# Attention and mixture-of-experts block: probabilities exchanged between SBUF quadrants for two groups at once, products four periods behind their scores

## The reference

```python
x = L0_attn_x
xn = _layernorm(x, axis=-1)
x = x + _L0_attn_ref(xn, ...) + _L0_ffn_ref(xn, ...)
# attention, 16 heads of 64, latent of 64:
q = x @ wq.T;  kv_latent = x @ w_kv_down.T;  k = kv_latent @ w_k_up.T;  v = kv_latent @ w_v_up.T
q = q * cos + _rotate_half(q) * sin;  k = k * cos + _rotate_half(k) * sin
scores = q @ k.T / 8, causal;  out = softmax(scores) @ v @ wo.T
```

## Time and profile before

| | us |
|---|---|
| median of 3 runs | 654.88 |
| lowest, highest | 654.70, 661.92 |
| the profiled execution | 649.8 |
| its span | 648.0 |
| TensorE busy in it | 557.0 |
| VectorE, ScalarE, GpSimd busy | 421.3, 391.6, 195.0 |

### The profile page before, as it was taken

One profiled execution on the slowest core, in us unless ns is written; L12 is line 12 of the kernel. 1 busy time (PEld: TensorE's weight loads), 2 busy tenths in 40 slices (PEclk: granted clock), 3 DMA queues, 4 the chain that ended last, 5 costly groups with the idle time before them and its releaser, 6 DMA issues.

```text
span 648.0 us, 13735 instructions
## 1 busy us (share of the span) xinstructions
PE 557.0 (86%) x4914; PEld 398.8 (62%) x4914; DVE 421.3 (65%) x921; ACT 391.6 (60%) x1036; POOL 195.0 (30%) x271
## 2 busy tenths in 40 slices
PE   2899999689988998799979988897889888877883
PEld 2666776446666666566656666675666656655663
DVE  6685364577775777477767776775777768654650
ACT  2562322356775676566666776774677767766771
POOL 3024030113432443133324432432343333211121
PEclk9899999789998999899999999998999999988996
DMA  9300014236767677666777777776768766876752
GB/s 256 106 1 1 1 22 109 69 94 203 185 193 199 208 188 195 184 186 194 207 191 221 188 201 214 212 192 187 211 195 222 191 205 182 210 205 194 208 194 73
DMA packets 63124, 108.45 MB, mean 167 GB/s; under 512 B 10561, under 2 KB 50385, under 8 KB 62929
## 3 DMA queue, kind: packets, MB, share of 16 engines
q1 hardware_dynamic: 60496, 106.13, 59.3%
q10 hardware_dynamic: 2560, 1.45, 0.9%
HBM read 47.78 MB, written 42.99 MB: 140 GB/s over the span
## 4 chain that ended last, share of the span: by engine, by line
PE 67%; DVE 13%; issue 9%; ACT 5%; DMA 4%; SPq 1%; DVEq 0%; POOLq 0%; ACTq 0%; POOL 0%
PE ps L452 21%; PE ps L413 20%; DVE prob_l L777 7%; PE ps L329 5%; PE ps L399 4%; PE ps L383 4%; DVE prod L657 3%; PE ps L463 3%; PE ps L437 2%; PE ps L331 2%; ACT prob_l L588 2%; ACT scaled L491 1%; DMA scratch<-zig 1%; PE ps L332 1%; PE ps L385 1%
## 5 line engine op out<-in xcount | busy, mean ns | idle before, releaser
L413 PE MATMUL ps<-qk 64*128 64x512 f32 (+3 forms) x768 | 160.6, 523 | 35.8 <-DVE negmax L777 34.4
L491 ACT ACTIVATE scaled<-ps,rden 128x128 f32<-128x128 f32 x256 | 73.2, 369 | 131.8 <-PE ps L463 131.8
L777 DVE CUSTOM_DVE_ANT_0 prob_l<-ps,mask 128x1024 f32<-128x1024 f32 (+3 forms) x128 | 126.0, 1022 | 39.1 <-PE ps L413 39.0
L837 POOL TENSOR_TENSOR roped<-prod 128x256 f32<-128x256 f32 x64 | 47.0, 735 | 321.8 <-DVE prod L657 321.8
L588 ACT ACTIVATE prob_l<-prob_l,negmax 128x1024 f32<-128x1024 f32 (+3 forms) x128 | 126.1, 1000 | 17.3 <-DVE negmax L777 17.3
L413 PEld LDWEIGHTS ps<-qk 64*128 64x128 f32 x768 | 64.4, 188 | 96.4 <-DVE negmax L777 47.5
L846 POOL TENSOR_TENSOR acc<-acc,scaled 128x256 f32<-128x256 f32 x128 | 93.0, 727 | 88.4 <-ACT scaled L491 83.2
L657 DVE TENSOR_TENSOR prod<-ps,rope 128x1024 f32<-128x1024 f32 x64 | 78.3, 1223 | 62.6 <-PE ps L332 31.8
L452 PE MATMUL ps<-fastT,lat 128*64 128x128 f32 x1280 | 88.9, 288 | 25.8 <-ACT slowT L491 11.6
L452 PEld LDWEIGHTS ps<-fastT,lat 128*64 128x64 f32 x1280 | 72.9, 142 | 54.3 <-issue 32.5
L790 DVE STREAM_TRANSPOSE zig<-prob_l 128x640 f32<-128x640 f32 x128 | 100.3, 822 | 0.0
(11 more groups left out here) (121 smaller groups left out, 593.4 us busy)
## 6 DMA issues: line engine op xcount, KB each, us to landing
scratch<-zig SPq DMA_DIRECT2D x64, 640.0 KB, 4.4
fastT<-scratch SPq DMA_DIRECT2D x256, 160.0 KB, 3.3
qk<-roped SPq DMA_DIRECT2D x64, 256.0 KB, 5.3
acc<-x SPq DMA_DIRECT2D x2, 512.0 KB, 5.4
rope<-c_rope SPq DMA_DIRECT2D x1, 1024.0 KB, 11.8
out<-acc SPq DMA_DIRECT2D x2, 512.0 KB, 4.1
wq_raw<-wq ACTq DMA_DIRECT2D x1, 512.0 KB, 7.3
wo_raw<-wo ACTq DMA_DIRECT2D x1, 512.0 KB, 8.5
```

Of the source, the lines that this page charges most:

```text
L413: mm = nc.tensor.matmul(to, qk[p][half, 0, rows], qk[p][half, 1, lo:hi], start=True, stop=True)
L491: return nc.scalar.activation(dst, src, ACT.Copy, scale=scale)
L777: nc.vector.tensor_tensor_reduce(row_sb(k, r), row_ps(k, r), mask[:, S - width:], -1.0, 3e38, ALU.add, ALU.min, accum_out=negmax[:, col:co ...
L837: nc.gpsimd.tensor_tensor(to[:, 0, :], x1[:, 0, :], x2[:, 1, :], ALU.subtract)
```

## The change

- The exchange no longer goes through DRAM. For two groups at once, 16 DMAs copy each square between partition quadrants directly, from `zig` to `fastT`, 32 partitions and 2560 bytes of each. `zig` and `fastT` hold two groups each and are doubled; `slowT` has four buffers in place of two.
- Products of group k are issued in iteration k + 4 (`LAG`) and its projection in iteration k + 5; before it was k + 1 and k + 2.
- On TensorE the products stand between long and short scores, right behind the projection of the group before, and the slow transposes behind the short scores.
- On ScalarE and VectorE the order is adapted; `turn_fast(k)` moves behind the long maxima of group k + 1.

```diff
-RING = 4
+RING = 8
+LAG = 4
...
-        zig = [sb(f"zig{s}", [P, 4, 2, FAST, 32], f32) for s in range(2)]
-        fastT = [sb(f"fastT{s}", [P, 4, 2, FAST, 32], f32) for s in range(2)]
-        slowT = [sb(f"slowT{s}", [P, 2, SLOW, P], f32) for s in range(2)]
+        zig = [sb(f"zig{s}", [P, 4, 2, 2, FAST, 32], f32) for s in range(2)]
+        fastT = [sb(f"fastT{s}", [P, 4, 2, 2, FAST, 32], f32) for s in range(2)]
+        slowT = [sb(f"slowT{s}", [P, 2, SLOW, P], f32) for s in range(4)]
...
-            def exchange(k):
-                s = k % 2
-                sp.wait_ge(zig_done, 2 * k + 2)
-                if k >= 2:
-                    sp.wait_ge(in_fast[s], READS * (k // 2))
-                sp.dma_start(scratch[s], zig[s][:].rearrange("p c a b n -> p c (a b n)")).then_inc(in_zig[s], 16)
-                sp.wait_ge(in_zig[s], 16 * (k // 2 + 1))
-                if k >= 2:
-                    sp.wait_ge(pv_done, k - 1)
-                by_query = scratch[s].rearrange("(q k) c n -> k q c n", q=4)
-                for ki in range(4):
-                    sp.dma_start(fastT[s][32 * ki:32 * ki + 32].rearrange("p c a b n -> p c (a b n)"),
-                                 by_query[:, :, ki, :]).then_inc(in_fast[s], 16)
+            def exchange(j):
+                s = j % 2
+                sp.wait_ge(zig_done, 4 * j + 4)
+                if j >= 2:
+                    sp.wait_ge(pv_done, 2 * (j - 1))
+                for turn_ in range(4):
+                    for qi in range(4):
+                        ki = (qi + turn_) % 4
+                        sp.dma_start(fastT[s][32 * ki:32 * ki + 32, qi],
+                                     zig[s][32 * qi:32 * qi + 32, ki]).then_inc(in_fast[s], 16)
...
-            for k in range(-1, GRPS - 1):
+            for k in range(-1, GRPS):
...
+                if k >= 0 and k % 2:
+                    exchange(k // 2)
...
-                exchange(k + 1)
...
             def products(k):
-                s, first = k % 2, QB * (unit_of(k) // QUADS)
+                s, first = k // 2 % 2, QB * (unit_of(k) // QUADS)
                 pe.wait_ge(slow_act, 2 * k + 2)
-                pe.wait_ge(in_fast[s], READS * (k // 2 + 1))
+                pe.wait_ge(in_fast[s], SWAPS * (k // 4 + 1))
                 if k:
                     pe.wait_ge(scaled_done, 4 * k)
...
-            for k in range(-1, GRPS + 2):
+            for k in range(-1, GRPS + LAG + 1):
                 if k + 1 < GRPS:
                     long_scores(k + 1)
-                if k >= 2:
-                    project(k - 2)
+                if k >= LAG + 1:
+                    project(k - LAG - 1)
+                if LAG <= k < GRPS + LAG:
+                    products(k - LAG)
+                if k + 1 < GRPS:
+                    short_scores(k + 1)
                 if 0 <= k < GRPS:
                     turn_slow(k)
-                if k + 1 < GRPS:
-                    short_scores(k + 1)
-                if 1 <= k <= GRPS:
-                    products(k - 1)
...
-            for k in range(-1, GRPS + 2):
-                if k >= 2:
-                    copy_output(k - 2)
-                    scale_rows(k - 2)
+            for k in range(-1, GRPS + LAG + 1):
+                if k >= LAG + 1:
+                    scale_rows(k - LAG - 1)
                 if k + 1 < GRPS:
                     softmax_exp(k + 1, 0)
                     softmax_exp(k + 1, 1)
+                if LAG <= k < GRPS + LAG:
+                    copy_output(k - LAG)
+                if k + 1 < GRPS:
+                    softmax_exp(k + 1, 2)
+                    softmax_exp(k + 1, 3)
                 if 0 <= k < GRPS:
                     copy_slow(k, 0)
                     copy_slow(k, 1)
-                if k + 1 < GRPS:
-                    softmax_exp(k + 1, 2)
-                    softmax_exp(k + 1, 3)
...
             def turn_fast(k, a):
                 dve.wait_ge(exp_done, 4 * k + a + 1)
-                if k >= 2:
-                    dve.wait_ge(in_zig[k % 2], 16 * (k // 2))
+                if k >= 4:
+                    dve.wait_ge(in_fast[k // 2 % 2], SWAPS * (k // 4))
...
-                if 0 <= k < GRPS:
-                    reciprocals(k)
+                if k >= 0:
+                    turn_fast(k, 0)
+                    turn_fast(k, 1)
                 if k + 1 < GRPS:
                     row_max(k + 1, 2)
                     row_max(k + 1, 3)
-                    turn_fast(k + 1, 0)
-                    turn_fast(k + 1, 1)
+                if k >= 0:
+                    reciprocals(k)
```

More of the change, by code:

```diff
@@ L80 @@
 STACK = 16 * 4
-READS = 16 * 4
+SWAPS = 16 * 16
 def block_kernel(nc, x, wq, w_down, w_kup, w_vup, wo, gate, e_up, e_down, s_up, s_down,
@@ L145, in block_kernel @@
         prob_s = [[sb(f"prob_s{s}{a}", [P, TB], f32) for a in range(2)] for s in range(2)]
-        zig = [sb(f"zig{s}", [P, 4, 2, FAST, 32], f32) for s in range(2)]
-        fastT = [sb(f"fastT{s}", [P, 4, 2, FAST, 32], f32) for s in range(2)]
-        slowT = [sb(f"slowT{s}", [P, 2, SLOW, P], f32) for s in range(2)]
+        zig = [sb(f"zig{s}", [P, 4, 2, 2, FAST, 32], f32) for s in range(2)]
+        fastT = [sb(f"fastT{s}", [P, 4, 2, 2, FAST, 32], f32) for s in range(2)]
+        slowT = [sb(f"slowT{s}", [P, 2, SLOW, P], f32) for s in range(4)]
         oT = [sb(f"oT{s}", [P, 2 * P], f32) for s in range(2)]
         scaled = [sb(f"scaled{s}", [P, 2, 2, P], f32) for s in range(2)]
-        scratch = [nc.dram_tensor(f"scratch{s}", (P, 4, 2 * FAST * 32), f32, kind="Internal").ap() for s in range(2)]
         ps = ctx.enter_context(nc.psum_tensor("ps", [P, 8, TB], f32))
@@ L193, in block_kernel @@
         rope_pe, rope_dve, rot_done, stored = map(sem, "rope_pe rope_dve rot_done stored".split())
-        in_zig = [sem("in_zig0"), sem("in_zig1")]
         in_fast = [sem("in_fast0"), sem("in_fast1")]
@@ L253, in _ @@
                     stack(n, 1)
-                if k == GRPS // 2 + 3:
+                if k >= 0 and k % 2:
+                    exchange(k // 2)
+                if k == GRPS // 2 + LAG + 3:
                     sp.wait_ge(ad_done, GRPS)
                     sp.dma_start(out_tiles[:, 0:QB, :], acc[:, 0:QB, :]).then_inc(stored, 16)
-                exchange(k + 1)
             sp.wait_ge(ad_done, 2 * GRPS)
@@ L450, in products @@
                         to = ps[HD * a:HD * a + HD, 6, (r // 2) * P:(r // 2 + 1) * P]
-                        probs = fastT[s][:, :, a, kb, :] if n is None else slowT[s][:, a, n, :]
+                        probs = fastT[s][:, :, k % 2, a, kb, :] if n is None else slowT[k % 4][:, a, n, :]
                         last = nc.tensor.matmul(to, lat[:, first + kb, :], probs, start=(at == 0),
@@ L458, in project @@
                 pe.wait_ge(o_done, k + 1)
-                pe.wait_ge(rope_dve, min(k + 13, PIECES * UNITS))
+                pe.wait_ge(rope_dve, min(k + LAG + 12, PIECES * UNITS))
                 for c in range(2):
@@ L467, in project @@
                             last.then_inc(proj_pe, 1)
-            for k in range(-1, GRPS + 2):
+            for k in range(-1, GRPS + LAG + 1):
                 if k + 1 < GRPS:
                     long_scores(k + 1)
-                if k >= 2:
-                    project(k - 2)
+                if k >= LAG + 1:
[4 more added lines that the diff above has]
+                    short_scores(k + 1)
                 if 0 <= k < GRPS:
                     turn_slow(k)
-                if k + 1 < GRPS:
-                    short_scores(k + 1)
-                if 1 <= k <= GRPS:
-                    products(k - 1)
                 for e in pieces_at(k):
-                    if k >= 2:
-                        pe.wait_ge(scaled_done, 4 * (k - 2) + 2)
+                    if k >= LAG + 1:
+                        pe.wait_ge(scaled_done, 4 * (k - LAG - 1) + 2)
                     pe.wait_ge(rope_dve, e)
@@ L592, in copy_slow @@
                 act.wait_ge(slow_pe, 2 * k + a + 1)
-                if k >= 2:
-                    act.wait_ge(pv_done, k - 1)
-                copy(slowT[k % 2][:, a], ps[:, 4 + a, :].rearrange("p (c n) -> p c n", c=SLOW)).then_inc(slow_act, 1)
-            for k in range(-1, GRPS + 2):
-                if k >= 2:
-                    copy_output(k - 2)
-                    scale_rows(k - 2)
+                if k >= 4:
+                    act.wait_ge(pv_done, k - 3)
+                copy(slowT[k % 4][:, a], ps[:, 4 + a, :].rearrange("p (c n) -> p c n", c=SLOW)).then_inc(slow_act, 1)
+            for k in range(-1, GRPS + LAG + 1):
+                if k >= LAG + 1:
+                    scale_rows(k - LAG - 1)
                 if k + 1 < GRPS:
@@ L787, in turn_fast @@
                 dve.wait_ge(exp_done, 4 * k + a + 1)
-                if k >= 2:
-                    dve.wait_ge(in_zig[k % 2], 16 * (k // 2))
-                nc.vector.transpose(zig[k % 2][:, :, a].rearrange("p c b n -> p b c n"),
+                if k >= 4:
```

(10 more changed lines are left out.)

## The result

| | before | after |
|---|---|---|
| median of the runs, us | 654.8 (650.0 to 661.9) | 676.4 (675.3 to 679.4) |
| the profiled execution, us | 649.8 | 675.3 |
| its span, us | 648.0 | 673.5 |

The ratio is 1.036, 95% interval 1.029 to 1.043: slower, clear of 2%. The prediction was 669, in a range of 658 to 682.

A forecast was written before the change was run, and what follows sets the result against it. TensorE, busy 86% of the span, was taken as the bound. Steady part +9.7, start −4.9 and end +12.0 gave +16.8 on 648.0: 664.8, or 666.6 with 1.8 around the span; 669 was taken, range 658 to 682.

The forecast's parts named there:

- The new wait: On TensorE, products wait for ScalarE's four scaled copies of the group before: 1.39 us more a period, 79 us in all.
- P to PV: On TensorE, time from the projection's start (P) to the products' start (PV): 1.96 us predicted in each period.
- The wait before S disappears: TensorE's wait for the long maxima before short scores (S) would be covered: 0.65 us less a period.
- No stall before products, no half clock in the steady part: The SBUF exchange would remove 33 us of DMA stalls and the half clock behind them on TensorE.
- Steady part: Long scores (L) of group 6 to 63: 48 periods of 8.24 us with rotary piece (R), nine of 7.45 without; +9.7 us.
- 8.1 to 8.4: Sign that the forecast is right: in the new trace, periods last 8.1 to 8.4 us.
- Small copies: 16 exchange DMAs per two groups, 0.65 us an issue, last landing at about 16 us, inside 22: no cost.
- The start: Groups 1 to 5, without projections, at VectorE's pace, 0.9 us saved ahead by earlier rotary products: −4.9 us.
- The end: After group 63's long scores, six projections and six products remain almost without cover, 4.62 us a round: +12.0 us.
- half-clock rival: Short idles bring half clock: at the end only, +10 to 679 us; far more in the steady part; 10%.
- Profiled time or median: The median before lay 5.1 us above the profiled time; 671.7 if common to both kernels, 666.6 if not; 669 taken.
- The exchange is late: Rival: beyond 16.5 us per pair of groups SP sets the pace; 790 us at 1.25 us an issue; 5%.

The follow-up runs named there:

- e1: The changed kernel with the projection's second half in bank 5 in place of bank 6, so products need not wait for the scaled copies: 594.5 us.
- e9: The changed kernel with the old TensorE and ScalarE order, five slowT buffers and the two-group exchange through DRAM: 632.4 us.
- e7: The kernel before, with the exchange in SBUF for each group by itself, 16 copies of 40 KB: 886.6 us.
- e10: e1 with LAG = 3 in place of 4: 651.0 us.
- e6: The changed kernel with the two DRAM tensors declared again but unused: 680.2 us.
- e8: e1 with the exchange for two groups through DRAM again: 625.7 us.
- e4: The changed kernel with the exchange for two groups through DRAM again, one store and four loads: 672.4 us.
- e2: The changed kernel with the slow transposes moved between projection and products on TensorE: 641.3 us.
- e3: The changed kernel with the old order of TensorE and ScalarE, keeping the lag of four and the SBUF exchange: 644.2 us.

## Why the prediction was right, point by point

- **The new wait.** Predicted P to PV 1.96 us in each period, measured 2.01 with 8 blocks, where the hop from ScalarE's end to TensorE's start is 0.15 us, not 0.06, and 2.08 with 6 and 5. Predicted 79 us in all; the profile names 88.3 before the products, 9.8 of them after L(63). e1 removes that wait and 82 us go. This is shown.
- **The wait before S disappears.** Yes: of 34.4 us 10.7 are left, in the first five groups. The two waits of 0.4 us before L are of the kind that the prediction priced in its periods without R.
- **No stall before products, no half clock in the steady part.** Yes, but I put it down to the route of the exchange, and e9 shows that the lag with two groups at a time does it on the old route too. My reading of the kernel before was also too broad: not each stall is followed by half clock. Of its nine between L(6) and L(63), four (0.6, 1.9, 2.4 and 2.9 us) were followed by a products block that started with 1.31 us.
- **Steady part.** Predicted 462.5 us from L(6) to L(63), measured 463.1. The period with 8 blocks took 8.26 us, where the terms give 8.31. So close a match is partly luck: P to PV was 2.05 in the mean, 0.09 more than predicted, while T (0.89) and R (0.80) were together 0.11 shorter. The 48 periods with R lasted 7.86 to 8.70 us each, wider than the 8.1 to 8.4 that I had named as a sign, and 8.23 in the mean.
- **Small copies.** Predicted 0.65 us an issue and the last landing about 16 us after the first issue. The issuing line of the changed kernel:

```profile
L233 SPq DMA_DIRECT2D fastT<-zig x512: 507/591/1681, 148.4 to 654.8; - x171
...
DMA to landing us min/median/max: 2.0/2.1/4.1
```

  Median 0.59 us, and 0.73 from one to the next when 16 follow each other, so some 12 us of issue and 2.1 to land: 14 us, inside the 22. With the stackings' share a pair of groups keeps SyncE busy for some 13 of 16.5 us. The limit of 16.5 us stands in the prediction only under a rival of 5%; e7 shows what comes beyond it, and e10 what comes with a period of lag less. Two remarks of mine do not hold. The `qk` row has one size only and cannot show a fixed part in a small DMA; here 80 KB land in 2.1 us and 256 KB in 4.3, in the median. And DMA time did not grow: the main queue took 40.0% of the 16 engines' span, against 59.3% before.
- **The start.** Predicted −4.9, measured −2.3. The 0.9 us that I gave to the earlier rotary product did not come: L(0) to L(1) took 13.6 us in both kernels. The rest is half clock, of which I had too little: with T and R slow from 140.1 on, the first of the five periods took 9.0 us in place of 7.9, and T at 159.9 ran slowly too. The mean granted clock from 117 to 168 us was 0.83.
- **The end.** Predicted +12.0, measured +13.3. Rounds took 4.77 us instead of 4.62, and the half-clock rival came in for one block. In e6, whose loop is the same, it came in for several and the end took 4.8 us more; so that rival was near, and the record does not say what decides it.
- **Ahead of the loop.** Predicted nothing, measured +4.1. The changed code is not reached there; see the last section. It is half of what the median lies above 669.
- **Profiled time or median.** I split the 5.1 us between the profiled execution of before and its median. The comparison of medians is 21.6 us, that of the profiled executions 25.5, of which 4.1 are that stretch ahead of the loop. That longer stretch may be in other runs of before as well, and missing from its profiled one; no profile shows it, so this stays open.

Of the rivals, none decided this kernel; half clock at the end came true in small part. "The exchange is late" was the one worth having: it decided e7, e8 and e10.

## What to carry to other kernels

When a block is moved to cover a wait, list for both of its new neighbours what they share: here a bank of PSUM, whose release (four copies of 1.14 us) had been covered by just the blocks that moved. An uncovered dependency costs its full latency in every period, and the cure can be another place for the result rather than another order. Lag hides a slow transfer up to its length in periods, so each improvement of the period uses up some of that cover, and has to be checked against it again. And when stalls on a transfer are few, look at what its queue issued just ahead: here it was always the same other transfer.

## What the runs showed that I had not expected

The 32 small projections at 20 us of the span ran at half the rate in the changed kernel. The group's line, and the window with its granted clock (after the engines' busy times; then DMA share and GB/s):

```profile
L296 PE MATMUL ps<-tokenT,xT 128*128 128x80 f32 x32 | 7.1, 423 | 0.7 <-ACT xT L488 0.7
...
20.00:30.00 10.00, 9.89 (x36) 8.34 (x37) 2.26 (x3) 3.23 (x5) 0.00 (x0) 0.50 0.00 0
```

Before they took 3.8 us. Of the twelve profiled executions here two have 3.8 (before and e4) and ten have 7.1, with the DRAM route or without it (e8, e9). The program up to there is the same in all twelve. In the changed kernel the granted clock was 0.50 in that window, the lower of its two levels (1.2 GHz). But the clock in the records does not settle it: in e2, e3, e6, e7 and e10 it reads 1.00 from 20 to 26 us, and the group took 7.1 us all the same. What decides it stays open.
